# A second image's neighbourhood attention laid between the tanh steps of the first

## What is computed

```
# 1. neighbourhood attention, 7 x 7 window, 8 heads of 16 channels
q, k, v = split(x @ qkv_w + qkv_b)
a   = softmax(q . k_near * hd**-0.5 + rpb)          # 49 neighbours
out = (a . v_near) @ proj_w + proj_b
y   = x + out * sigmoid(relu(x @ g1_w + g1_b) @ g2_w + g2_b)
t   = layernorm(y) * ln_g + ln_b
# 2. additive attention inside an image (L = 1024 rows, U = 32 units)
n   = layernorm(t)
h   = tanh(q[:, i, None] + k[:, None, j] + bh)      # L x L x U
t   = t + softmax(h . Wa + ba) @ n
# 3. eight experts of 512 hidden units, one chosen per row, 320 rows each at most
t   = t + ffn(layernorm(t))
```

## Time and profile before

| | us |
|---|---|
| median of three runs | 749.13 (749.04 to 751.52) |
| the profiled execution's own time | 750.55 |
| its span, first to last instruction | 748.7 |
| PE, DVE, ACT, POOL busy | 538.8, 557.1, 588.1, 419.6 |
| first scores of the rounds' loop | 31.63 |
| last values of the second image end | 169.4 |
| first tanh starts, last ends | 177.35, 662.1 |

### The profile page before, as it was taken

One profiled execution on the slowest core, in us unless ns is written; L12 is line 12 of the kernel. 1 busy time (PEld: TensorE's weight loads), 2 busy tenths in 40 slices (PEclk: granted clock), 3 DMA queues, 4 the chain that ended last, 5 costly groups with the idle time before them and its releaser, 6 DMA issues.

```text
span 748.7 us, 12070 instructions
## 1 busy us (share of the span) xinstructions
PE 538.8 (72%) x4516; PEld 267.9 (36%) x4516; DVE 557.1 (74%) x1316; ACT 588.1 (79%) x398; POOL 419.6 (56%) x453
## 2 busy tenths in 40 slices
PE   6889998885357676775675876666767756777894
PEld 3656665661012131221221222222312212246683
DVE  3567689887986878878878788879788788752256
ACT  2377776654379999999999999999999999941341
POOL 2000000006448888878878878878888788710365
PEclk9999999998679999999999999999999999998898
DMA  9500000007000000000000000000000000004101
GB/s 321 172 3 1 2 2 2 2 1 295 0 1 0 5 12 1 12 3 9 12 1 12 11 1 13 12 1 13 11 1 12 4 9 11 1 13 128 29 16 33
DMA packets 13786, 22.24 MB, mean 30 GB/s; under 512 B 1232, under 2 KB 10994, under 8 KB 12960
## 3 DMA queue, kind: packets, MB, share of 16 engines
q1 hardware_dynamic: 12320, 18.56, 7.2%
q0 software_dynamic: 1408, 2.91, 1.2%
HBM read 14.73 MB, written 7.37 MB: 30 GB/s over the span
## 4 chain that ended last, share of the span: by engine, by line
issue 33%; ACT 30%; PE 17%; DVE 12%; DMA 2%; POOL 1%; POOLq 0%; DVEq 0%; SPq 0%; ACTq 0%
ACT arena L807 28%; PE ps L475 3%; PE ps L726 2%; PE ps L488 2%; DVE arena L884 2%; PE ps L716 2%; PE ps L457 2%; DVE arena L1033 2%; DMA arena<-xbuf 1%; ACT pm L811 1%; PE ps L514 1%; PE ps L601 1%; PE ps L506 1%; DVE arena L893 1%; PE ps L498 1%
## 5 line engine op out<-in xcount | busy, mean ns | idle before, releaser
L378 POOL TENSOR_SCALAR arena<-k,q 128x1024 f32<-128x1024 f32 (+1 forms) x384 | 371.3, 984 | 265.4 <-DVE q L1011 169.4
L807 ACT ACTIVATE arena<-arena 128x4096 f32<-128x4096 f32 x128 | 451.0, 3602 | 23.9 <-DVE arena L1033 23.9
L601 PE MATMUL ps<-arena,cst 128*32 128x512 f32 x2048 | 256.0, 620 | 166.2 <-ACT arena L807 161.6
L1033 DVE TENSOR_SCALAR arena<-ps,q 128x512 f32<-128x512 f32 (+1 forms) x256 | 248.1, 1012 | 63.4 <-PE ps L601 57.3
L601 PEld LDWEIGHTS ps<-arena,cst 128*32 128x32 f32 x2048 | 55.3, 111 | 323.2 <-ACT arena L807 232.8
L762 ACT ACTIVATE arena<-arena,mn 128x320 f32<-128x320 f32 (+1 forms) x128 | 62.6, 539 | 33.4 <-DVE mn L884 32.2
L884 DVE CUSTOM_DVE_ANT_0 arena<-ps,arena 128x320 f32<-128x320 f32 (+1 forms) x128 | 53.1, 471 | 15.6 <-PE ps L457 11.0
L475 PE MATMUL ps<-cst,arena 128*128 128x128 f32 x352 | 54.8, 287 | 3.8 <-ACT arena L769 3.8
L475 PEld LDWEIGHTS ps<-cst,arena 128*128 128x128 f32 x352 | 40.6, 147 | 13.7 <-ACT arena L769 6.7
L769 ACT ACTIVATE arena<-ps 128x512 f32<-128x512 f32 x56 | 32.9, 587 | 9.2 <-PE ps L475 9.2
L624 PE MATMUL ps<-x_one,ptm 128*128 128x129 f32 x256 | 37.3, 289 | 0.0
(11 more groups left out here) (134 smaller groups left out, 582.0 us busy)
## 6 DMA issues: line engine op xcount, KB each, us to landing
arena<-in_w SPq DMA_DIRECT2D x2, 2048.0 KB, 10.7
xbuf<-rec SPq DMA_DIRECT2D x1, 2720.0 KB, 13.9
arena<-xbuf SPq DMA_DIRECT2D x1, 1440.0 KB, 8.0
arena<-in_inner SPq DMA_DIRECT2D x1, 1280.0 KB, 10.9
arena<-in_b SPq DMA_DIRECT2D x1, 1280.0 KB, 15.6
tokens<-in_xT SPq DMA_DIRECT2D x4, 256.0 KB, 6.2
arena<-in_top SPq DMA_DIRECT2D x1, 1024.0 KB, 7.2
arena<-in_bottom SPq DMA_DIRECT2D x1, 1024.0 KB, 14.9
```

The costliest lines, as they stand in the source:

```text
L378: last = nc.gpsimd.tensor_scalar(ring[t % 3][:, c, 0:n], k4[:, img * L:img * L + n], q4[:, m:m + 1], 1.0, ALU.add, ALU.mult)
L601: last = nc.tensor.matmul(bank(half)[c * U:(c + 1) * U, :], c_("wa", U - QPG - QPG * s, 2 * U - QPG - QPG * s), ring[t % 3][:, c, half * 5 ...
L807: nc.scalar.activation(ring[t % 3], ring[t % 3], ACT.Tanh).then_inc(h_ready, 1)
L1033: last = nc.vector.tensor_scalar(ring[t % 3][:, c, lo:L], keys[:, lo:L], q4[:, m:m + 1], None, ALU.add)
```

## The change

The first image's 16 rounds stay ahead of the tanh steps. The second image's rounds go into the tanh loop: round rho begins at step 3 (rho - 17), so round 16 at step -3, round 17 at step 0 and round 31 at step 42. Its scores are made in two pairs in banks 2 and 3, its chunks are all turned into bank 4 between the two halves of a step's energies, and all are copied by VectorE one step later. Its projections for queries and keys lie in the seam between the stages, its values in steps 0 to 2, its blocks' sums, spread and projection three or four steps after the values. Two regions, `front` and `late`, with `back`, replace the arena, so that the ring doesn't overlay what late rounds still read.

For image 0 the keys of VectorE's sums lie in bank 5 alone: VectorE adds 2 x 512 columns a step and GpSimd 1024, 1024, 512 and 512. For image 1 the split is as before.

The norm is made from `bn_stats` and `bn_aggr` for each row block: blocks 0 to 3 and 8 to 11 with the scaling by GpSimd (`scale_rows`, `weigh_rows`, `normal_rows`), blocks 4 to 7 and 12 to 15 on VectorE. Blocks 0 to 3 are done in rounds 9 to 15, 4 to 7 in the seam, 8 to 11 at steps 28 to 38, 12 to 15 at steps 49 to 58. The gate's hidden units are made the other way round (units on partitions), with its relu on ScalarE and its sum on TensorE. The two halves of a main block's turns share bank 4. A main block's router steps and scatter come two to four steps earlier than before, so that the last block alone is left after the last tanh. SP loads the experts' weights after the last late values, at step 47, and fetches the sorted tokens in six DMAs; the weights of the router are taken in two halves.

```diff
--- before.py
+++ after.py
@@ -32,6 +32,8 @@
 PW = CHUNKS[INNER] * P
 VB = 12
 NR = 2 * NB
+RPI = NR // B
+PACE = 3
 U = 32
...
+def begin(rho):
+    return PACE * (rho - RPI - 1)
...
+def turn_step(rho, c):
+    return begin(rho) + 3 + c
...
+def values_step(rho):
+    return begin(rho) + 3 + CHUNKS[kind_of(rho // 2)]
...
+def project_step(j):
+    t = values_step(2 * j + 1)
+    return t + (3 if j == NB - 1 or (t + 4) % CH == 6 else 4)
...
             fetch(xe, 0, 3, 0, C, ld_xe[0])
             fetch(xe, 3, 5, 0, C, ld_xe[1])
-            fetch(xr, 0, TILES, C, REC, ld_xr)
-            fetch(xe, 5, TILES, 0, C, ld_xe[2])
+            fetch(xe, 5, 10, 0, C, ld_xe[2])
+            fetch(xr, 0, 10, C, REC, ld_xr[0])
+            fetch(xe, 10, TILES, 0, C, ld_xe[3])
+            fetch(xr, 10, TILES, C, REC, ld_xr[1])
...
+            pool.wait_ge(ld_rest, 16)
+            scale_rows(1, 0, 4)
+            weigh_rows("lng", ALU.mult, 0, 4)
+            weigh_rows("lnb", ALU.add, 0, 4, done=True)
+            normal_rows(1, 0, 4)
...
             def key_query_sums(t):
                 i, s = divmod(t, CH)
                 img = i // BPI
+                if t < 2:
+                    pool.wait_ge(pv_done, RPI)
                 if t == 0:
-                    pool.wait_ge(n_ready, NG * NR)
                     pool.wait_ge(k4_ready, 2)
                     pool.wait_ge(q4_ready, 1)
...
+                for c in range(4 if img == 0 else 3):
+                    lo, hi = (0, L) if c < 2 else (L // 2, L) if img == 0 else (0, L // 2)
                     m = i * U + c * CH + s
-                    last = nc.gpsimd.tensor_scalar(ring[t % 3][:, c, 0:n], k4[:, img * L:img * L + n], q4[:, m:m + 1],
+                    last = nc.gpsimd.tensor_scalar(ring[t % 3][:, c, lo:hi], k4[:, img * L + lo:img * L + hi], q4[:, m:m + 1],
                                                    1.0, ALU.add, ALU.mult)
                 last.then_inc(pool_sums, 1)
@@ -387,19 +516,24 @@
...
+                if t == first + 4:
+                    scale_rows(2, 8, 12)
+                if t == first + 5:
+                    weigh_rows("lng", ALU.mult, 8, 12)
+                if t == first + 6:
+                    weigh_rows("lnb", ALU.add, 8, 12, done=True)
+                if t == first + 10:
+                    normal_rows(2, 8, 12)
...
+            def score_pair(rho, pair):
+                pe.wait_ge(n_ready, NG * rho + 2 * pair)
+                for g in range(2 * pair, 2 * pair + 2):
+                    last = score(rho, g, 2 + g % 2)
+                last.then_inc(pair_done, 1)
...
+            def turn_probs_late(rho, c):
+                if c == 0:
+                    pe.wait_ge(p_ready, NG * (rho + 1))
+                pe.wait_ge(turn_copied, probs_before(rho, c))
+                for g in range(NG):
+                    last = nc.tensor.transpose(bank(4, g * P, (g + 1) * P), prob[rho % 2][:, g, c * P:(c + 1) * P],
                                                c_("ident"))
-                last.then_inc(pt_done, 1)
...
+            value_rows(0, 6).then_inc(v_done, 1)
+            pe.wait_ge(q_ready, 4)
+            pe.wait_ge(k_ready, 1)
+            scores(0)
+            value_rows(1, 7).then_inc(v_done, 1)
             pe.wait_ge(v_ready, 1)
-            value_rows(2, 6)
-            pe.wait_ge(q_ready, 4)
+            value_rows(2, 6).then_inc(v_done, 1)
+            pe.wait_ge(v_ready, 2)
+            gate_rows(7)
+            gate_sums(7)
             pe.wait_ge(k_ready, 2)
-            scores(0)
...
+            for t in range(begin(RPI), END):
+                rho = round_at(t, begin)
+                if rho is not None:
+                    if rho == RPI:
+                        pe.wait_ge(q_ready, 8)
+                        pe.wait_ge(k_ready, 4)
+                    score_pair(rho, 0)
+                if t == begin(RPI):
+                    turn_tokens(1, 1)
+                    key_half(1, 1)
+                    query_columns(0, 0)
...
+                rho = round_at(t, values_step)
+                if rho is not None:
+                    values_late(t, rho)
...
+            heads_out(BPI - 1)
...
+            tokens_out(1, 1)
+            keys_out(1, 1)
+            act.wait_ge(q4_done, 1)
+            nc.scalar.activation(q4[:, 0:L // QPG], bank(0, 0, L // QPG), ACT.Identity, bias=c_("bh")).then_inc(q4_ready, 1)
...
+            for t in range(begin(RPI), END):
+                if 0 <= t < T:
+                    hidden_units(t)
+                p = query_block(t, 1)
+                if p is not None:
+                    soften_main(p)
+                rho = round_at(t - 1, begin)
+                if rho is not None:
+                    soften(rho, (0, 1))
+                rho = round_at(t - 2, begin)
+                if rho is not None:
+                    soften(rho, (2, 3))
...
+            def turned_late(rho, c):
+                dve.wait_ge(turn_done, probs_before(rho, c) + 1)
+                if rho < RPI + 2:
+                    dve.wait_ge(pv_done, rho - 1)
+                else:
+                    dve.wait_ge(sixth_done, sixth_writes(values_step(rho - 2)) + 1)
+                nc.vector.tensor_copy(pts[rho % 2][:, c, :], bank(4)).then_inc(turn_copied, 1)
...
+            inverse(BPI - 1)
+            scale_end(0, 4, ln_last)
+            scaled(BPI - 1)
+            dve.wait_ge(y_ready, BPI - 1)
+            row_stats(4, BPI - 1)
+            gated(BPI - 1)
+            dve.wait_ge(y_ready, BPI)
+            row_stats(BPI - 1, BPI)
+            scale_start(4, BPI)
+            scale_end(4, BPI)
+            normal_rows(y_all, 4, BPI)
+            weigh_rows(4, BPI)
+            row_stats(4, BPI)
+            scale_start(4, BPI)
+            scale_end(4, BPI)
+            normal_rows(x_all, 4, BPI)
+            dve.sem_inc(t_ready[1], 1)
...
+                    dve.wait_ge(k4_ready, 4)
                     dve.wait_ge(q4_ready, 2)
-                keys = ps[:, 2 * 512:4 * 512]
                 for c in range(2, QPG):
...
+                    at = (5 if img == 0 else 2) * 512
                     m = i * U + c * CH + s
-                    last = nc.vector.tensor_scalar(ring[t % 3][:, c, lo:L], keys[:, lo:L], q4[:, m:m + 1], None, ALU.add)
...
+            for t in range(begin(RPI), END):
+                if turn_at(t - 1):
+                    turned_late(*turn_at(t - 1))
...
+                    least(p)
+                if 0 <= t + 2 < T:
+                    key_query_sums(t + 2)
+                rho = round_at(t, begin)
+                if rho is not None:
+                    bias_pair(rho, 0)
+                rho = round_at(t - 1, begin)
+                if rho is not None:
+                    bias_pair(rho, 1)
+                if 0 <= t < 3:
+                    dve.wait_ge(turn_done, turn_uses(t) + 1)
+                    value_rows(3 + t, 4)
+                    dve.wait_ge(v_ready, 4 + t)
+                    dve.sem_inc(turn_copied, 1)
+                rho = round_at(t, values_step)
+                if rho is not None and rho % 2:
...
+                if t == late_rows + 5:
+                    normal_rows(x_all, 12, NB)
+                    dve.sem_inc(t_ready[3], 1)
```

1094 lines of the change are left out of this document (627 added, 467 removed).

## The result

The changed kernel takes 742.62 us (median of 4 runs, 739.52 to 744.08), the kernel before 750.18 in the same comparison: ratio 0.989, 95% interval 0.986 to 0.993. It is faster by 1.1%, where 5.6% were forecast (707 us, range 689 to 731). Ratios and intervals, here and with the experiments, leave out executions in a slower state (two of ten of `router_later`, one of four of `roots_on_pool`); the medians hold all. The profiled execution has a span of 741.9 us.

What follows compares the result with a forecast made beforehand. ScalarE was taken to bound the tanh stage, TensorE and handshakes the first. Start and seam -63.9, tanh stage +25.6, tail -4.3 gave -42.6 from 750.55: 708.0, as median 707 us, range 689 to 731.

Steps and rivals of the forecast that it cites:

- Parts 1 to 3: Start, first image's rounds and seam: first tanh at 113.4 instead of 177.35, 63.9 us gained.
- Part 2: Stage one: half the rounds leave, 72.4 us go; norm beside rounds 9 to 15 costs 2 us.
- rival (c): Seam longer than costed, small chained VectorE instructions at 0.6 to 0.8 instead of 0.17: 12 us more, 719; chance 0.08.
- Part 5: Loads and tail: TensorE's wait of 4.32 us for tokens goes, 4.3 gained, tail 82; later weight loads cost nothing.
- Part 4: Tanh stage: stays ScalarE's, floor 494.4 us plus 16 for added waits, 510.4 in all, 25.6 lost.
- 5 for rows 8 to 11: Tanh stage: 5 us added over the floor for these rows' norm, 8.6 us of VectorE with 0.23 a step free.
- 3 for rows 12 to 15: Tanh stage, steps 49 to 62: 3 us added for some 18 us of norm with about 1 us free a step.
- The shared port: VectorE beside GpSimd's sums: row scalings slow from 0.34 to 0.79 us; no such slowing taken for the rounds.
- (b): Rival: VectorE sets the pace of steps with rounds, 5.0 us instead of 4.56; 21 more, 728; chance 0.15.
- (d): Rival: GpSimd's four sums stretch from 3.58 to 4.92 us a step; 37 more, 744; chance 0.06.
- (e): Rival: VectorE and TensorE take turns over bank 4, 5.96 us a step; 67 more, 774, slower; chance 0.04.
- the signs named ahead: Tanh stage: ScalarE over 96% busy, last tanh about 624, step 4.3 to 4.7; wrong if ScalarE's waits exceed 25 us.

Runs made afterwards that it cites:

- router_later: The changed kernel with turning, logits and counts of a block's router one, two and three steps later, and the scatter at phase 13: 753.26 us.
- roots_on_pool: The changed kernel with the inverse roots of rows 8 to 11 moved from VectorE to GpSimd: 743.81 us.
- no_late_norm: The changed kernel without the norm of the first image's rows 8 to 15 on VectorE and GpSimd, signals kept: 709.58 us.
- pool_yields: The changed kernel with seven added waits: GpSimd holds its next sums until VectorE has ended that step's root chain: 732.60 us.
- no_pool_rows: The changed kernel without GpSimd's scaling and weighting of rows 8 to 11, signals kept: 744.01 us.
- temps_in_psum: The changed kernel with the root's two temporaries for rows 12 to 15 in a free PSUM bank instead of SBUF: 736.05 us.
- one_sbuf_input: The changed kernel with every VectorE norm instruction for rows 12 to 15 given at most one SBUF input, order kept: 734.94 us.

## Why the prediction was wrong

**Parts 1 to 3 (start, seam) held.** First inner scores at 18.82 for 20.2. The 2 us of Part 2 for the norm beside the rounds did not come: 64.7 us for the rounds, and the last head copy at 83.85. The chain from there is 25.9 us for 25.8. First tanh at 109.79 for 113.4. The 25.8 hold 2 us for a lower clock of TensorE, an estimate of mine: in the kernel before, sixteen energy products took 3.64 us at a granted clock of 0.50 (from 193.06 on) and 1.92 at 1.00 (from 232.57 on). In the kernel after the clock was 0.66 from 96 to 100 us and 0.50 from there to 117.3; no run shows what that alone cost. It and GpSimd's norm of rows 0 to 3 together cost no more than allowed; rival (c) did not come in this place, and its small instructions at 0.6 to 0.8, and longer, came in another.

**Part 5 held.** The tail is 82.05 for 82.3, and the wait of the earlier trace rows is gone.

**Part 4 failed, in the 16 us added over ScalarE's floor; 55.7 were measured.** The floor itself was right: steps 0 to 15 run at it, and the 3 us for the first steps were not even needed. Measured against each term: 3 for the start, none, at a granted clock of 0.50 up to 117.3 us; 4 for handshakes in 45 steps, 5 in steps 16 to 31 alone; 5 for rows 8 to 11, about 18 (14 of them vanish with the norm); 3 for rows 12 to 15 and 1 for steps 48 to 63, 27 and 3 more behind them. Of these, 17 vanish with the norm and 10 stay: there GpSimd, with 3.52 us a step and a scatter of 1.0 in every eighth for a floor of 3.64, has hardly any reserve, and in no_late_norm the router's row still waits up to 5.03 us behind it. How the 10 divide is not shown.

**The step that failed is "The shared port", and with it the 3 us for rows 12 to 15.** I looked at how much longer large instructions take beside GpSimd's sums, found eight scalings at 0.79 us for 0.34, and put 3.6 us, which are in the 18 for rows 12 to 15. That these eight alone would be slowed was my estimate; the runs show more. Two things were wrong. The small instructions of the root were priced at 0.17 from a row in which GpSimd was idle, though they too have two SBUF inputs or both ends in SBUF. And I took the price of a collision to be the rest of one GpSimd instruction (0.79 for 0.34), whereas it can be eight of them (7.01 us) or the whole rest of GpSimd's run (11.19 us), though in other places it was again one (0.62 to 1.06). The 24 instructions took 20.0 us where 4.0 is plain, and the 16 more are about the 17 that vanish with the norm in steps 48 to 63. The change itself made GpSimd's runs nearly endless, by giving it a fourth sum: 3.52 us for a step of 3.52 to 3.64. I had checked that sum only against ScalarE's time, as GpSimd's own bound.

**A second term failed, for another reason: the 5 us for rows 8 to 11, which cost 14.** That is more than the whole plain time of VectorE's share, 8.6. Waiting beside GpSimd's sums explains little of it (2.5 us of waiting; 3.9 us gained in pool_yields); GpSimd's own norm work explains none (no_pool_rows). What remains, some 10 us, goes when the norm leaves the rounds; whether it was the clock, VectorE's plain time or the handshakes stays open.

What the runs show is the place of the operands: with the root's temporaries in SBUF its small instructions took up to 7.01 us (after), with them in PSUM 0.17 at most (rows 12 to 15 in temps_in_psum and one_sbuf_input). Waiting for one GpSimd instruction to end doesn't cover the 7.01 and 11.19 us: eight and more of them ran in each. Why VectorE was passed over at their ends, and let in at others, no run shows.

**The rivals.** (b), VectorE as pace at 5.0 a step, did not come: steps 8 to 15 took 4.25. (d), GpSimd's sums stretched to 4.92, came within 2 us of the time, 744, by luck: the sums keep 3.52, and it is VectorE that stands still. (e), two engines in series at 5.96 a step, was passed in the four steps 32 to 35 around the 5.72 us wait (6.6 to 8.2 us each), but not as a steady state. Of the signs named ahead, several showed: ScalarE's waits exceeded 25 us (41.8), it was busy 90% of the stage and not over 96%, the last tanh ended at 659.85 and not at 624, and the mean step up to 47 was 4.73, just outside 4.3 to 4.7. GpSimd's sums did not grow (1.12 and 0.69 a piece).
